# Attention of a transformer layer: groups of four score tiles in place of three, eight exponential tiles, and less scratch memory

## The reference

```python
q, k, v = (einsum('bsm,hmd->bhsd', x, kernel[n]) for n in range(3))   # x: 4 x 1024 x 256, 16 heads of 64
attn = softmax(einsum('bhsd,bhtd->bhst', q, k) * (1 / (64 * 64 * 16)))
x = layernorm(x + einsum('bsf,fm->bsm', heads(attn @ v), WO))
x = layernorm(x + mixture_of_experts(x))      # 8 experts, the top 2 of each token, hidden size 1024
```

## Time and profile before

| | us |
|---|---|
| median of three runs | 1883.01 (1877.25 to 1883.25) |
| the profiled execution: its own time | 1879.8 |
| its span, first to last instruction | 1878.0 |
| TensorE busy in the span | 1757.6 (94%) |
| VectorE busy | 1385.4 (74%) |
| ScalarE busy | 1046.4 (56%) |
| attention's slots, from the first score to the last values | 37.41 to 1158.04 |
| a slot with three units | 17.75 |

### The profile page before, as it was taken

How to read it: one execution, slowest core, us unless ns; L and a number is a source line. 1 busy time by engine, 2 the same in 40 slices (tenths; PEclk the granted TensorE clock), 3 DMA queues, 4 the chain that set the end, 5 groups by cost and what they waited for, 6 DMA issues and landing times. The chain is left out here.

```text
span 1878.0 us, 31867 instructions
## 1 busy us (share of the span) xinstructions
PE 1757.6 (94%) x10909; PEld 1193.3 (64%) x10909; DVE 1385.4 (74%) x2213; ACT 1046.4 (56%) x1554; POOL 353.7 (19%) x399
## 2 busy tenths in 40 slices
PE   6999999999999999999999997987659999999986
PEld 5555555555555555555555553877549999999982
DVE  5888888888888888888888887555566655566647
ACT  5555555565555555555655654544455544455537
POOL 1000000000000000000000000011127766666654
PEclk9999999999999999999999998998879999999998
DMA  5011111111111111311111112444123333233335
GB/s 173 29 46 35 35 46 35 35 41 40 34 35 45 36 35 40 127 34 40 40 35 40 40 35 86 146 157 157 55 91 90 88 80 77 59 87 89 87 49 178
DMA packets 80198, 127.09 MB, mean 68 GB/s; under 512 B 12753, under 2 KB 46737, under 8 KB 77777
## 3 DMA queue, kind: packets, MB, share of 16 engines
q1 hardware_dynamic: 61808, 98.27, 15.6%
q0 software_dynamic: 18272, 27.31, 7.3%
HBM read 86.72 MB, written 38.83 MB: 67 GB/s over the span
## 5 line engine op out<-in xcount | busy, mean ns | idle before, releaser
L450 ACT ACTIVATE a_e<-banks 128x1024 f32<-128x1024 f32 x512 | 490.4, 1026 | 334.9 <-PE banks L346 334.9
L559 DVE TENSOR_TENSOR a_esum<-a_esum,a_e 128x1024 f32<-128x1024 f32 x384 | 470.4, 1225 | 80.5 <-ACT a_e L450 52.9
L360 PE MATMUL banks<-a_e,a_v 128*64 128x512 f32 x2048 | 481.6, 602 | 0.0
L360 PEld LDWEIGHTS banks<-a_e,a_v 128*64 128x64 f32 x2048 | 130.0, 136 | 251.2 <-issue 227.6
L346 PE MATMUL banks<-a_qh,a_kh 64*128 64x512 f32 x1024 | 222.8, 432 | 5.3 <-issue 5.3
L63 POOL MEMSET ident<- 128x128 f32 x1 | 0.2, 204 | 1139.9 <-POOLq L112 1139.9
L346 PEld LDWEIGHTS banks<-a_qh,a_kh 64*128 64x128 f32 x1024 | 96.2, 184 | 173.4 <-issue 107.9
L346 PE MATMUL banks<-a_qh,a_kl 64*128 64x512 f32 x1024 | 202.4, 391 | 0.0
L1790 ACT ACTIVATE e_g<-banks,e_b1c 128x256 f32<-128x256 f32 x280 | 114.9, 471 | 154.1 <-PE banks L1737 152.9
L346 PE MATMUL banks<-a_ql,a_kh 64*128 64x512 f32 x1024 | 200.2, 388 | 0.0
L1750 PE MATMUL banks<-e_w2h,e_hh 128*128 128x256 f32 x560 | 162.3, 290 | 4.5 <-issue 1.9
(11 more groups left out here) (232 smaller groups left out, 3294.4 us busy)
## 6 DMA issues: line engine op xcount, KB each, us to landing
attn_out<-a_ot SPq DMA_DIRECT2D x64, 256.0 KB, 2.0
a_inv<-inv_rows SPq DMA_DIRECT2D x126, 128.0 KB, 2.9
a_w<-w_qkv SPq DMA_DIRECT2D x32, 256.0 KB, 3.1
raw<-attn_out SPq DMA_DIRECT2D x4, 2048.0 KB, 8.8
t_ot<-attn_out SPq DMA_DIRECT2D x4, 2048.0 KB, 8.2
raw<-w_up SPq DMA_DIRECT2D x8, 1024.0 KB
raw<-w_down SPq DMA_DIRECT2D x8, 1024.0 KB
raw<-x_t SPq DMA_DIRECT2D x8, 512.0 KB, 9.3
```

What stands on the lines that cost most here:

```text
L360: mm = pe.matmul(o_acc[h * DH:(h + 1) * DH, :], v[quad % 2][:, n, head], e[(slot * ST + n) % NE][:, h * BANK:(h + 1) * BANK], start=n == 0 ...
L450: act.activation(e[t % NE], ring[n % RING], ACT.Exp, scale=SCALE).then_inc(e_ok, 1)
L559: dve.tensor_tensor(acc[:, :], acc[:, :], e[(slot * ST + n) % NE], ALU.add).then_inc(add_ok, 1)
```

## The change

The tiles of a slot are grouped as 4 and 4, and a slot's order on TensorE becomes: scores 0 to 3; values 4 to 7 of the previous slot; scores 4 to 7; the units; values 0 to 3. There are eight exponential tiles `e` instead of six. What stood behind the second or third group now stands behind the second of two: on ScalarE `act_rows_high` and the evacuations, on VectorE `normalize` (behind addition 7 instead of addition 5), `dve_rows_low` and the evacuations. The ring in PSUM stays at three entries. To find the SBUF for two more `e` tiles, `e_turned` goes (the turned sums are put in the other slot's `esum`), and `o_raw`, `quarter`, `quarters`, `total_e` and `inv_e` become parts of the weight tile `wv`, which is free after the opening. Three waits are added or moved for that.

```diff
-    NE = 6
+    NE = ST
...
-        o_raw = sb("a_o_raw", [P, BANK])
-        e_turned = sb("a_e_turned", [P, S])
-        quarter = sb("a_quarter", [P, QT])
-        quarters = sb("a_quarters", [QT, P // QT, QT])
-        total_e = sb("a_total_e", [QT, QT])
-        inv_e = sb("a_inv_e", [QT, QT])
+        o_raw = wv[:, 0, :, :].rearrange("p a c -> p (a c)")
+        quarter = wv[:, 1, 0, 0:QT]
+        quarters = wv[0:QT, 1, 1, :].rearrange("c (j q) -> c j q", q=QT)
+        total_e, inv_e = (wv[0:QT, 1, n, 0:QT] for n in (2, 3))
...
-        GROUPS = [range(0, 3), range(3, 6), range(6, ST)]
+        GROUPS = [range(0, HALF), range(HALF, ST)]
...
             for slot in range(SLOTS):
-                for j, group in enumerate(GROUPS):
-                    for n in group:
-                        scores(slot, n)
-                    for u in units(slot) if j == 2 else ():
-                        pe_unit(pe, u)
-                    if j:
-                        for n in GROUPS[j - 1]:
-                            values(slot, n)
-                    elif slot:
-                        for n in GROUPS[-1]:
-                            values(slot - 1, n)
-            values(SLOTS - 1, ST - 2)
-            values(SLOTS - 1, ST - 1)
+                for n in GROUPS[0]:
+                    scores(slot, n)
+                for n in GROUPS[1] if slot else ():
+                    values(slot - 1, n)
+                for n in GROUPS[1]:
+                    scores(slot, n)
+                for u in units(slot):
+                    pe_unit(pe, u)
+                for n in GROUPS[0]:
+                    values(slot, n)
+            for n in GROUPS[1]:
+                values(SLOTS - 1, n)
             sums(SLOTS - 1)
...
                 if slot:
                     act.wait_ge(o_ok, slot)
-                act.copy(o_raw[:, :], o_acc).then_inc(o_copied, 1)
+                else:
+                    act.wait_ge(wvl_ok, 2)
+                act.copy(o_raw, o_acc).then_inc(o_copied, 1)
...
-                    for u in units(slot) if j == 2 else ():
+                    for u in units(slot) if j == 1 else ():
                         act_evacuate(act, u)
...
                 if n == 1:
-                    if slot >= 2:
-                        dve.wait_ge(turned_ok, (slot - 2) * TURNS + 1)
+                    if slot:
+                        dve.wait_ge(turned_ok, (slot - 1) * TURNS + 2)
...
-                dve.transpose(e_turned[:, :], esum[slot % 2][:, :]).then_inc(turned_ok, 1)
+                dve.transpose(esum[(slot + 1) % 2][:, :], esum[slot % 2][:, :]).then_inc(turned_ok, 1)
...
                 if slot == SLOTS - 1:
                     dve.wait_ge(sum_done, 1)
+                    dve.wait_ge(o_ok, slot)
...
-                    for u in units(slot) if j == 2 else ():
+                    for u in units(slot) if j == 1 else ():
                         dve_evacuate(dve, u)
```

More of the change, by code:

```diff
@@ L255, in spread @@
                 sp.wait_ge(turned_ok, (slot + 1) * TURNS)
-                sp.dma_start(inv_rows[slot].rearrange("(c q) -> c q", q=QT), inv_e[:, :]).then_inc(inv_kept, 16)
+                sp.dma_start(inv_rows[slot].rearrange("(c q) -> c q", q=QT), inv_e).then_inc(inv_kept, 16)
                 sp.wait_ge(inv_kept, 16 * (slot + 1))
@@ L564, in inverses @@
                 dve.wait_ge(add_ok, slot * ADDS + ADDS)
-                dve.transpose(e_turned[:, :], esum[slot % 2][:, :]).then_inc(turned_ok, 1)
+                dve.transpose(esum[(slot + 1) % 2][:, :], esum[slot % 2][:, :]).then_inc(turned_ok, 1)
                 dve.wait_ge(turned_ok, n + 1)
-                dve.tensor_reduce(quarter[:, :], e_turned[:, :].rearrange("p (c k) -> p c k", k=QT), AX.X, ALU.add)\
+                dve.tensor_reduce(quarter, esum[(slot + 1) % 2][:, :].rearrange("p (c k) -> p c k", k=QT), AX.X, ALU.add)\
                    .then_inc(turned_ok, 1)
@@ L572, in inverses @@
                 dve.wait_ge(turned_ok, n + TURNS - 2)
-                dve.tensor_reduce(total_e[:, :], quarters[:, :, :].rearrange("c j q -> c q j"), AX.X, ALU.add)\
+                dve.tensor_reduce(total_e, quarters.rearrange("c j q -> c q j"), AX.X, ALU.add)\
                    .then_inc(turned_ok, 1)
@@ L577, in inverses @@
                     dve.wait_ge(inv_kept, 16 * slot)
-                dve.reciprocal(inv_e[:, :], total_e[:, :]).then_inc(turned_ok, 1)
+                dve.reciprocal(inv_e, total_e).then_inc(turned_ok, 1)
             def normalize(slot):
@@ L589, in normalize @@
                     dve.wait_ge(ot_out[slot % 2], 16 * (slot // 2))
-                dve.tensor_tensor(ot[slot % 2][:, :], o_raw[:, :], inv[:, :], ALU.mult).then_inc(o_ok, 1)
+                dve.tensor_tensor(ot[slot % 2][:, :], o_raw, inv[:, :], ALU.mult).then_inc(o_ok, 1)
             for slot in range(SLOTS):
```

## The result

The changed kernel takes 1867.05 us (median of six runs, 1863.93 to 1870.72) against 1882.58 for the kernel before on the same chip (six runs): a ratio of 0.9924, with a 95% interval of 0.9907 to 0.9942. The forecast was 1868 in a range of 1859 to 1880, and faster.

What follows compares the result with a forecast made beforehand. Attention was taken to be bound by TensorE's matmul stream. Saved switches of 21.7 us, less stalls of 6.5 and 0.3 for first and last slot, gave -14.9 us: 1868 against the 1883.0 median, range 1859 to 1880.

Steps and rivals of the forecast that it cites:

- What bounds: In attention, slots 1 to 62, TensorE is busy all 1095.99 us; a slot lasts as long as its matmuls.
- The gain per round, 0.35: Each round of scores and values spends 0.35 us on switching; one round fewer saves 21.7 us over slots 1 to 62.
- The waits: TensorE's waits for exponentials at fourth tiles and first unit: about 0.05 us in odd slots, 0.17 in even; 6.5 in sum.
- the rival with slow releases: Releases after exponentials take 0.10 us instead of 0.05; the sum becomes -9.3 us, 1874; chance 0.15.
- the gain is eaten: Each of three TensorE waits costs 0.11 us on top, 0.33 a slot; 1888 us at most; chance 0.12.
- slower: Waits dry out TensorE's queue, each of three costing 0.20 to 0.3 us beyond ScalarE's lateness; 1898 us; chance 0.08.
- No stall at all: Weight loads go ahead without harm and even slots' exponential isn't late: -21.4 us, 1862; chance 0.12.
- First and last slot: Slot 0 takes 16.2 us instead of 17.34, the last slot 1.37 more than 15.05; together about +0.3 us.
- What was costed at nothing: Six points on VectorE, ScalarE, SyncE's queue, `o_acc`, `e` tiles and turned sums, each taken to cost nothing.
- `spread` and `store` wait for a `normalize` some 4 us later: In SyncE's queue, the weight transfer behind them gets 4 us less lead, but its data is used later; no cost.
- the cover of 1.6 us: VectorE's new k ends at 15.8 us, the next slot starts at 17.4; with two units the cover is 0.3.
- The sum: Over the kernel, -21.7 + 6.5 + 0.3 = -14.9 us; set against the median of 1883.0, the forecast is 1868.

Runs made afterwards that it cites:

- the memory part alone: Changed kernel's memory layout with the old order of three groups (3, 3, 2), against the kernel before: 1870.32 us against 1869.15, ratio 0.9999.
- the conversion's edit: Changed kernel with ScalarE's weights' conversion ahead of the output's copy: 1850.50 us, on another chip 1863.50; ratios to the kernel before 0.9904 and 0.9900.
- the extra copies: Changed kernel with two more small ScalarE copies ahead of tile 4's exponential, all slots but the first: 1916.50 us, ratio 1.0256 to the kernel before.

## Why the prediction was right, point by point

**What bounds.** Attention's TensorE stream, and nothing else: the memory part alone brought nothing, one round more cost 24 to 26 us, and the stretch behind attention kept its 720.0 us.

**The gain per round, 0.35.** Right: rounds cost 0.35 in the changed kernel (four tiles of each kind take 2.98 + 3.58 = 6.56 us, and 6.56 - 4 x (0.69 + 0.86) = 0.36, of which 0.02 is the wait at the fourth tile) and 0.38 to 0.41 with four rounds.

**The waits.** Forecast: 0.05 in odd slots, 0.17 in even. The two groups of scores should be 2.96 each without waits and take 2.98 and 3.00 (odd), 2.98 and 3.12 (even): 0.06 and 0.18. The 0.12 in even slots comes from ScalarE's order, as the conversion's edit showed by removing it, and lateness passes one for one, as the extra copies showed. The release took 0.05, so the rival with slow releases is out; "the gain is eaten" and "slower" fall too, as a restarted stream pays nothing beyond the lateness. "No stall at all" is out by the same groups, since 2.98 to 3.12 isn't 2.96. The page of the Trainium skill that the prediction named, "Advanced Engine Details and Errata", section Network/Comms, gives 50-100 ns for reading a semaphore's value from a sequencer; the releases in the trace agree with its lower end.

**First and last slot.** Forecast 16.2 and 15.05 + 1.37 = 16.42; measured 53.53 - 37.05 = 16.48 and 1144.86 - 1128.38 = 16.48, together 0.3 more than forecast.

**What was costed at nothing.** Right except once. The step "`spread` and `store` wait for a `normalize` some 4 us later" left out that behind slot 40 the early loads delay the inverses. `normalize` has always waited for them there, 1.43 us before, 2.29 in the changed kernel:

```profile
776.40 0.69 DVE L590 TENSOR_TENSOR a_ot<-a_o_raw,a_inv 128x512 f32<-128x512 f32 x1 [1.43 <-DMA a_inv<-inv_rows]
```

```profile
770.96 0.69 DVE L590 TENSOR_TENSOR a_ot<-a_wv,a_inv 128x512 f32<-128x512 f32 x1 [2.29 <-DMA a_inv<-inv_rows]
```

```profile
772.91 0.50 PE L344 MATMUL banks<-a_qh,a_kh 64*128 64x512 f32 x2 [0.55 <-DVE a_kl L495]
```

It now stands nearer to k, and TensorE starts slot 42 0.6 us late. The price is small, but it is the one place where the cover of 1.6 us ran out. With the early loads behind slot 59 this wait is gone, which shows that they are its cause.

**The sum.** Forecast -14.9, measured in attention -12.8, of which slots 1 to 62 have -13.4 instead of -15.2. Of that 1.8, 0.6 is the stall above. 1.1 is in the units, which take 4.31 us in odd and 4.34 in even slots instead of 4.30. Why isn't settled: in a second execution of the same kernel they took 4.30 and 4.31, with the conversion first 4.29, so it moves from one execution to another. The medians differ by 15.5, 2.7 more than attention; the runs of one kernel spread over 6 to 7 us, so this is no more than chance may give. That the median came within 1 us of the forecast is therefore in part luck: attention gained 2.1 us less than forecast, and the medians happen to differ by 2.7 more than attention does. The mechanism and its terms are what was right, to 2.1 of 14.9 us.

## What to carry to other kernels

A TensorE that is busy all the time can still hold time to win: take distances between starts for groups of different length, and what doesn't grow with the group is the price of switching. Before a group is made longer, put the consumer's chain (start of the first consumer, its rate, its duration, the release) beside the producer's rate: here a ring of three carries four tiles at the price of 0.02 us; each tile beyond takes ScalarE's 0.92 us instead of 0.69, and an exponential that starts 0.12 late costs 0.12. And whatever is put into a queue should be judged by everything that stands behind it, not by the one transfer one has in mind.

## What the runs showed of the hardware

One kernel differs by some 13 us between chips (kernel before: 1869.15 and 1868.32 us on two chips, 1881.74 on a third and 1882.58 where the result was measured), and the traces put this behind attention, in stages that no edit touches. From the end of the last values to the end of the span it is 720.0 us in both traces from where the result was measured and 718.6 to 722.1 in the four from the third chip, but 706.8 to 710.8 in the eight from the two chips with 1869.15 and 1868.32 (the memory part alone has 1869.2 - 1160.38 = 708.8). What makes the difference isn't known from these runs. And behind a stop of 2.99 us TensorE's next 5.42 us ran at a granted clock of 0.50.
